# One paired slot and an eight-slot first stage in the first FFN of a macaron block

## The reference, cut to what matters

```python
x = L0_attn_h                                   # 2 sequences x 2048 tokens x 256
x = x + 0.5 * ffn(layernorm(x), ...)            # first FFN
x = x + recurrence(layernorm(x), ...)           # down, 3 gated linear recurrences, up
x = x + 0.5 * ffn(layernorm(x), ...)            # second FFN, the same weights

def ffn(x, Wr, br, ln_g, ln_b, W1, b1, W2, b2):   # 8 experts, F = 1024
    idx = argmax(softmax(x @ Wr + br))             # one expert for a token
    gate = max(softmax(x @ Wr + br))
    h = relu(layernorm(x)*ln_g+ln_b  @ W1[idx] + b1[idx])
    return gate * (h @ W2[idx] + b2[idx])
```

## Time and profile before

| what | value |
|---|---|
| median of 3 runs | 701.4 us (701.39 to 705.12) |
| profiled execution | 700.31 us, of which the span is 698.5 us |
| PE busy | 642.4 us, 92% of the span |
| DVE busy | 412.0 us, 59% |
| ACT busy | 268.1 us, 38% |
| POOL busy | 168.6 us, 24% |
| granted PE clock, mean of the run | 0.967 of full speed |

### The profile page before, as it was taken

The page is one execution under the profiler, slowest core; times in us unless marked ns, Lnnn a source line. Parts: engine busy times, 40 slices in busy tenths (PEclk is TensorE's granted clock), DMA queues, the critical chain, the costliest instruction groups (busy, mean ns, idle before and its releaser), DMA issues.

```text
span 698.5 us, 15261 instructions
## 1 busy us (share of the span) xinstructions
PE 642.4 (92%) x4294; PEld 550.9 (79%) x4294; DVE 412.0 (59%) x1446; ACT 268.1 (38%) x639; POOL 168.6 (24%) x174
## 2 busy tenths in 40 slices
PE   7549999999999999999998998999979899999993
PEld 5448988999988878898677867879878888786782
DVE  7756673333356586777787684877756762344331
ACT  4204221323245557553571644744442311233220
POOL 4633433111121120133312341104411331111111
PEclk9659999999999999999998999999999999999998
DMA  8969876845464463436415436434274445767640
GB/s 284 315 206 388 276 255 207 275 166 203 161 205 147 156 204 107 134 128 189 168 55 198 147 117 223 137 98 153 87 260 145 132 173 192 236 210 257 235 151 18
DMA packets 62512, 129.25 MB, mean 185 GB/s; under 512 B 8010, under 2 KB 39253, under 8 KB 62293
## 3 DMA queue, kind: packets, MB, share of 16 engines
q1 hardware_dynamic: 55940, 111.25, 47.8%
q0 software_dynamic: 6480, 16.92, 6.6%
HBM read 109.10 MB, written 19.96 MB: 185 GB/s over the span
## 4 chain that ended last, share of the span: by engine, by line
PE 63%; DVE 15%; issue 8%; DVEq 6%; POOL 3%; DMA 2%; ACT 1%; POOLq 0%; ACTq 0%; SPq 0%
PE bank L1935 27%; PE bank L1969 24%; PE bank L1907 2%; DVE st L856 2%; POOL routed_rows L743 2%; DVEq L454 2%; PE bank L1926 2%; PE bank L1961 2%; DVE rec L1253 1%; DVE act_t L1369 1%; DVE y_b L1387 1%; PE bank L1824 1%; DVE rec L1229 1%; PE bank L1831 1%; PE bank L1762 1%
## 5 line engine op out<-in xcount | busy, mean ns | idle before, releaser
L1935 PE MATMUL bank<-mn_t,w 128*128 128x128 f32 x2176 | 268.4, 280 | 8.3 <-DVE act_t L1369 4.7
L1935 PEld LDWEIGHTS bank<-mn_t,w 128*128 128x128 f32 x2176 | 258.1, 196 | 20.6 <-issue 11.5
L1969 PE MATMUL bank<-w,act_t 128*128 x1088 | 254.8, 383 | 5.7 <-DVE y_b L1387 5.3
L1969 PEld LDWEIGHTS bank<-w,act_t 128*128 128x128 f32 x1088 | 200.2, 191 | 43.0 <-issue 19.3
L1626 ACT ACTIVATE mn_t<-bank,vec 128x128 f32<-128x128 f32 x146 | 58.9, 456 | 224.2 <-PE bank L1907 224.2
L1369 DVE TENSOR_SCALAR act_t<-bank,vec 128x128 f32<-128x128 f32 x272 | 76.7, 345 | 80.2 <-PE bank L1935 66.7
L1654 ACT ACTIVATE act_t<-bank,vec 128x128 f32<-128x128 f32 x272 | 77.7, 368 | 61.3 <-PE bank L1935 61.1
L752 POOL DMA_INDIRECT x_middle<-res,pay x37 | 36.9, 999 | 217.1 <-DVE res L1394 176.7
L1387 DVE TENSOR_TENSOR y_b<-bank,b_all 128x256 f32<-128x256 f32 x68 | 28.9, 425 | 92.0 <-PE bank L1969 81.6
L752 POOL DMA_INDIRECT out_x<-res,pay x34 | 34.0, 999 | 197.2 <-DVE res L1394 153.0
L743 POOL DMA_INDIRECT routed_rows<-rows,dest x64 | 63.9, 998 | 58.0 <-PE bank L1935 28.2
(11 more groups left out here) (249 smaller groups left out, 530.2 us busy)
## 6 DMA issues: line engine op xcount, KB each, us to landing
w<-in_L_ffn_W SPq DMA_DIRECT2D x82, 1024.0 KB, 5.3
pay<-routed_rows SPq DMA_DIRECT2D x72, 130.0 KB, 2.1
rows<-in_L_attn_h SPq DMA_DIRECT2D x8, 512.0 KB, 6.8
rows<-x_middle SPq DMA_DIRECT2D x8, 512.0 KB, 5.0
rec<-in_L_ffn_W SPq DMA_DIRECT2D x3, 1024.0 KB, 7.3
routed_rows<-fill SPq DMA_DIRECT2D x2, 1040.0 KB, 7.7
routed_rows<-rows,dest POOLq DMA_INDIRECT x64, 3.5
b_all<-in_L_ffn_b SPq DMA_DIRECT2D x1, 1024.0 KB, 11.5
```

The costliest lines, as they stand in the source:

```text
L1935: last = t.matmul(b_hid[half][:, c % 4 * P:(c % 4 + 1) * P], w1[u % W1S][:, k * F + c * P:k * F + (c + 1) * P], mn_t[p][i % 2][:, k * P:(k ...
L1969: last = t.matmul(b_out[i % 2], act_t[i % 2][:, c * P:(c + 1) * P], w2[:, ds(eb * (WE // FC) + c * D, D)], start=c == 0, stop=c == FC - 1)
```

## The change

The first FFN's first stage has eight slots in place of nine, and its second stage has one paired slot (slot 12). Everything that hangs on the first FFN's first stage moves up by one slot: the rows of the first chunk are read back after slot 16 and not 17, and the numbers of this chunk's chain fall by 48 (192 on PE). The scatters of the third and fourth chunk stand 24 units apart in place of 48. DVE now works out `pairs` twice, once for each FFN: for the first at 168 and 169, ahead of the second table, which moves by 24. In the second FFN the three parts of `pairs`, and the parts of the last table, are spread over two and a half slots.

```diff
-LN_POW = [984, 1272, 1705, 2161]
+LN_POW = [936, 1272, 1705, 2161]
...
-R_SCATTER = [[[None, None, None, None], [None, None, None, None], [72, 120, 168, 216], [264, 312, 360, 408]],
-    [[1560, 1608, 1656, 1704], [2040, 2088, 2136, 2160], [2472, 2520, 2568, 2616], [2856, 2904, 2952, 3000]]]
-TABLE_PARTS = [[[None, None, None, None, None, None], [169, 192, 240, 264, 288, None]], [[1584, 1609, 1633, 1682,
-    1683, 1728], [2066, 2088, 2112, 2113, 2116, 2281], [2497, 2544, 2568, 2569, 2593, 2616], [2881, 2904, 2905,
-    2952, 2953, None]]]
+R_SCATTER = [[[None, None, None, None], [None, None, None, None], [72, 96, 120, 144], [192, 216, 240, 264]],
+    [[1512, 1560, 1608, 1656], [2040, 2088, 2136, 2160], [2472, 2520, 2568, 2616], [2856, 2904, 2952, 3000]]]
+TABLE_PARTS = [[[None, None, None, None, None, None], [192, 216, 240, 264, 288, None]], [[1536, 1561, 1585, 1634,
+    1635, 1680], [2066, 2088, 2112, 2113, 2116, 2281], [2497, 2544, 2568, 2569, 2593, 2616], [2928, 2929, 2952,
+    2953, 2976, None]]]
...
-PAIR_PARTS = [2880, 2880, 2880]
+PAIR_PARTS = [[168, 168, 169], [2880, 2904, 2905]]
...
-    PAIRS = 3
-    HALVES = 2 * PAIRS
-
-    EARLY = ((FULL,), (4, 9, 9))
+    PAIRS = (1, 3)
+
+    EARLY = ((FULL - 1,), (4, 9, 9))
...
-    PAIR_AT = [[], [FIRST[1][-1] + 2 + 3 * k for k in range(PAIRS)]]
-
-    WITH = (FULL + E, (TH + PART) // P, (T - T // NC + PART) // P)
+    PAIR_AT = [[FIRST[0][-1] + k for k in (4,)], [FIRST[1][-1] + k for k in (2, 5, 8)]]
+
+    WITH = (EARLY[0][0] + PAIRS[0] + E - 1, (TH + PART) // P, (T - T // NC + PART) // P)
...
+                    if is_pair(0, i + 1):
+                        pair_second_weights(0, i + 1)
...
-                    for part in range(3):
-                        if k == PAIR_PARTS[part]:
-                            pairs(part)
+                    for f in range(FFNS):
+                        for part in range(3):
+                            if k == PAIR_PARTS[f][part]:
+                                pairs(f, part)
...
+                        if is_pair(0, i - 1):
+                            activate_pair(0, i - 1)
```

More of the change, by code:

```diff
@@ L55 @@
+R_RANKS = [[None, None, 216, 552], [6000, 7944, 9936, 11472]]
+R_PLACE = [[None, None, 48, 144], [1488, 2017, 2472, 2856]]
+R_COUNTS = [[None, None, 288, 696], [6096, 8160, 10008, 11544]]
+R_KEEP_COUNTS = [[None, None, 73, 168], [1513, 2065, 2496, 2880]]
 R1_TRANSPOSE = [0, 48]
@@ L278, in macaron_block, with words @@
         later = sb("later", [P, LATER], I32)
[L279 to L285, removed]
+        WORDS = [[sum(COUNT[p])] * 3 + [2 * PAIRS[p]] * 2 + [PAIRS[p], 1] for p in range(FFNS)]
+        tab = sb("tab", [P, sum(map(sum, WORDS))], I32)
+        def words(p, n):
+            at = sum(map(sum, WORDS[:p])) + sum(WORDS[p][:n])
+            return tab[:, at:at + WORDS[p][n]]
+        tab_row, tab_b, tab_off, pair_row, pair_b, pair_off, tab_used = (
+            [words(p, n) for p in range(FFNS)] for n in range(7))
         pay = [[sb(f"pay{i}_{s}", [P, RW]) for s in range(RING)] for i in range(2)]
@@ L631, in between_passes @@
                         for i in range(W1S):
-                            last = max(j for j in range(u) if j % W1S == i)
-                            sp.wait_ge(m_h[0], 2 * last + 2)
+                            last = max(j for j in range(u) if any(load % W1S == i for load in loads_of(0, j)))
+                            sp.wait_ge(m_h[0], halves_before(0, last) + 2)
                             next_weights(1, i)
@@ L966, in keep_counts, with pairs @@
                 dve.drain()
-            def pairs(part):
+            def pairs(f, part):
+                n = 2 * PAIRS[f]
                 every = cnt_c[:, NC - 1, :]
@@ L972, in pairs @@
                 order = beyond_s[:, 0:E * E].rearrange("p (e k) -> p e k", e=E)
-                of = jump_s[:, 0:HALVES * E].rearrange("p (h e) -> p h e", e=E)
-                of_row = beyond_s[:, E * E:E * E + HALVES * E].rearrange("p (h e) -> p h e", e=E)
-                row, short, by = (a[:, 0:HALVES] for a in (slot_v, slot_c, slot_r))
-                sq, of_all = [P, E, E], [P, HALVES, E]
+                of = jump_s[:, 0:n * E].rearrange("p (h e) -> p h e", e=E)
+                of_row = beyond_s[:, E * E:E * E + n * E].rearrange("p (h e) -> p h e", e=E)
+                row, short, by = (a[:, 0:n] for a in (slot_v, slot_c, slot_r))
+                sq, of_all = [P, E, E], [P, n, E]
                 if part == 0:
@@ L1014, in pairs @@
                     v.tensor_reduce(short, of_row, AX.X, ALU.add)
-                    v.tensor_scalar(pair_row, by, 0.0, None, ALU.max)
+                    v.tensor_scalar(pair_row[f], by, 0.0, None, ALU.max)
                     v.tensor_tensor(row, row, by, ALU.subtract)
                     dve.drain()
-                    v.tensor_scalar(pair_b, short, -float(FC), float(E * FC), ALU.mult, ALU.add)
+                    v.tensor_scalar(pair_b[f], short, -float(FC), float(E * FC), ALU.mult, ALU.add)
                     by_half = row.rearrange("p (k h) -> p k h", h=2)
@@ L1037, in tables @@
                 i0 = FIRST[f][s]
-                slots = i0 + PAIRS if f and last else i0
+                slots = i0 + PAIRS[f] if last else i0
                 rw, tb, of = (t[f][:, i0:i0 + n] for t in (tab_row, tab_b, tab_off))
@@ L1340, in norm @@
                 if is_pair(p, i):
[L1341 to L1342 removed]
+                    n = PAIR_AT[p].index(i)
+                    off = pair_off[p][:, n:n + 1]
                 else:
@@ L1351, in activate_pair @@
             def activate_pair(p, i):
-                experts = [expert_of_half(dve, i, h) for h in range(2)]
+                experts = [expert_of_half(dve, p, i, h) for h in range(2)]
                 dve.wait_ge(m_h[p], halves_before(p, i) + 4)
@@ L1634, in activate_pair @@
             def activate_pair(p, i):
-                experts = [expert_of_half(act, i, h) for h in range(2)]
+                experts = [expert_of_half(act, p, i, h) for h in range(2)]
                 act.wait_ge(m_h[p], halves_before(p, i) + 3)
```

114 lines of the change are left out of this document (54 added, 60 removed).

## The result

The changed kernel takes 719.8 us (median of 4 runs, 716.9 to 726.8), the kernel before 703.3 on the same chip (4 runs, 701.4 to 705.3): ratio 1.024, 95% interval 1.018 to 1.029. It is 2.4% slower, and the range given, 697.3 to 705.3, doesn't hold it. The profiled execution took 718.47 us with a span of 716.7 us, 18.2 more than before.

A forecast was written before the change was run, and what follows sets the result against it. PE, busy 92% of the span, was taken as the bound, with DVE's list setting the pace between the FFNs. Terms +1.4 +4.3 -3.2 +0 -2.3 gave +0.2 us, forecast 701.6 us, range 697.3 to 705.3.

The forecast's parts named there:

- The first chunk a slot earlier: First chunk's chain meeting other parts of the second chunk's: 0 us, with 1.5 on both sides.
- Scatters priced at 0: POOL's scatters, four at a time before the eighth slot: nothing on PE waits for them earlier, so 0 us.
- `pairs` ahead of finish: First FFN's slots 3 to 5: new PE waits of 3.0 and 2.4 us, the old 1.32 goes; sum +4.3 us.
- The paired slot: First FFN's slot 12: a pair and two slots take 23.12 us against 21.75 for three ordinary slots; +1.4 us.
- The handover: End of first FFN: DVE's list is the bound, so the dropped slot gives back 3.2 us, not 7.25.
- a whole slot of 7.25: Rival at the handover: if DVE doesn't hold it, the full -7.25 us comes back, 697.5 us; chance 0.25.
- The spread: Second FFN, slots 18 to 19: spreading `pairs` and last table cuts a loss of 5.6 us to 3.3; -2.3 us.
- the clock stays down: Rival: half rate after the 3.0 us wait, second product of slot 3 onward; +4.6 us, 706.2; chance 0.17.

The follow-up runs named there:

- e8: Changed kernel with the second half of the first chunk's chain (from its second layer's projection on) put back a place later; 708.2 us, ratio 1.004.
- e10: Changed kernel with only the gates of the first chunk's third layer moved later on PE, behind the first product's second half; 713.5 us, ratio 1.016.
- e6: Kernel before with only the scatters of the third and fourth chunk drawn together, 24 units apart; 707.2 us, ratio 1.005.
- e2: Changed kernel with all numbers of the first chunk's chain put back a place later, as before; 710.8 us, ratio 1.009.
- e5: e2 with the scatters of the third and fourth chunk 48 units apart again, the last one 24 after the seventh; 710.9 us, ratio 1.006.
- e3: Kernel before with only the second FFN's `pairs` and last table spread as in the changed kernel; 700.9 us, ratio 0.996.
- e7: e5 with the first FFN's `pairs` parts 1 and 2 later (192, 193) and its second table at 216 to 312; 712.8 us, ratio 1.009.
- e9: e7 with nine first-stage slots as in the kernel before, one paired slot kept, last scatter at 408; 705.8 us, ratio 1.003.
- e1: The changed kernel run again, unaltered; 720.7 us, ratio to the kernel before 1.023.
- e12: e3 with part 1 of the first FFN's second table behind its slot's activation (216 instead of 192); 700.6 us, ratio 0.995.
- e11: The kernel of e3 again, on the same chip as e9; 701.9 us, ratio to the kernel before 0.998.

## Why the prediction failed

Of its six terms four came out near their size; two that it set at nothing held the loss. In the traces the stretches add up to +15.9 us without what lies ahead of the first store, for a forecast of +0.2: slots 0 to 10 +8.5, the pair +1.4, slots 16 to 34 +11.0, the handover -2.0, the second FFN -2.9.

- **The first chunk a slot earlier: "0, with 1.5 on both sides". This is the step that failed.** It measured +11.0 (slots 16 to 34). I asked with whom the chain's parts would meet, and not what PE does between two links of the chain. Work of the other chunk, bound to its own places, had covered 3.2 us in one gap and 1.7 in the next; when the chain moved against it, the gaps lay open (e8, e10), and half rate behind the first cost 2.7 us more.
- **Scatters priced at 0: failed too.** "Nothing on PE waits for them earlier" was beside the point: drawn together they cost 6.0 us in slots 0 to 10 alone (e6) and 6.4 in slot 3 of the changed kernel. Which of the two failed terms weighs more in the time is clear all the same: putting the chain back gave 9.9 us (e2), taking the scatters apart nothing that shows (e5), since DVE's waits open instead.
- **`pairs` ahead of finish, +4.3: right in its mechanism, in its size partly by luck.** It measured +5.0 in e5, with waits of 2.26 and 2.44 for 3.0 and 2.4; the one of 1.64 that goes (e3) leaves 3.1, and 1.8 are half rate, for which the prediction added nothing. In the changed kernel the two waits are 0.42 and 2.69, and only about 2 us of the term shows, since the stall of slot 3 had made PE late already. Terms at one place don't add.
- **The paired slot, +1.4: right**, +1.4 in all kernels that have it.
- **The handover, -3.2: nearly right**, -2.0 here, -2.7 to -2.9 in e2, e5, e7, e8 and e9, but -0.8 in e1, and 1.2 of it moves without a change. That a whole slot of 7.25 doesn't come back held in all. PE's idle time there grows as forecast, from 2.6 to 5.8 us; that DVE's list is the reason wasn't tested, and two of the waits are on ACT (1.26 and 0.96).
- **The spread, -2.3: right**, -2.4 in its stretch and -2.7 from turn to turn (three slots take 24.8 us for 27.5); its new waits are 1.06, 0.52 and 0.59, and the loss left is 3.0 for the 3.3 expected.
- **The clock.** The rival "the clock stays down" had the slower side, but put it behind the wait for `pairs`. Half rate did come, behind the stall of slot 3 and the wait of 3.18. The rule of the Trainium skill that I cited (TensorE: Matmul & The Clock Gate, section Why this matters for your kernels) is to leave no long gap between bursts; e10, with a gap of 1.40 in place of 3.18, agrees. My reading of it, that waits near 2 us are harmless, was too mild: half rate follows a wait of 1.96 in e9 and one of 2.11 in e12 (last section).

The range was too narrow because the chain's term was given the spread of small waits seen before, the scatters' none at all, and a term for moving work against other work had no bound from the size of what might lie open: the 5.4 us between spread and gates could have been read from the trace of before.

## What to carry to other kernels

When a dependent chain is moved against a second one, list for each of its round trips to another engine what the waiting engine does meanwhile; if that work stays where it is, the trip's full length is the bound, not 0. A slot less is worth only what the engine that sets that slot's pace gets back: here 1 to 3 us of 7.25, and `pairs`, the pair and the waits used that up. Take each part of a bundled change alone first; the spread was the one that paid.

## What the runs showed of the hardware

In six of six traces indirect DMAs drawn together (73 to 81 us) were followed by gaps of 0.3 to 1.2 us on PE in slot 3, in none of eight with them apart; why, and when a second group does it too, is open. And the length of a wait alone doesn't settle whether the clock falls: e11 and e12 have the same code at the second FFN's third stage and nearly the same wait, yet only e12 drops. PE timelines of e11 and of e12:

```profile
515.53 0.41 PE L1907 MATMUL bank<-ident,mn 128*128 128x128 f32 x2 [2.14 <-issue]
515.77 1.89 PE L1969 MATMUL bank<-w,act_t 128*128 x8
```

```profile
516.33 0.66 PE L1907 MATMUL bank<-ident,mn 128*128 128x128 f32 x2 [2.11 <-issue]
516.78 3.33 PE L1969 MATMUL bank<-w,act_t 128*128 x8
```

The same 8 matmuls take 1.89 us in one and 3.33 in the other, and e12 is 1.6 us later from there on. In the first FFN, waits of 2.67 to 2.77 us ahead of the second product of slot 4 are followed by 16 matmuls in 3.72 us in four traces (after, e1, e2, e8), one of 2.71 in e10 by 16 in 5.40, and one of 1.96 in e9 by 16 in 5.40 too. Such places may be part of why runs of one kernel lie up to 12 us apart here; this wasn't measured, since only one run of each has a trace.
